# Softplus as one activation in a selective-scan block, its projections one pair earlier

## The chip, the cores and the metric

One Trainium2 chip, one of its cores. The time is the device time of one execution in microseconds (us), the median of several.

## The reference

Input x is (8, 512, 128). The block is x + 0.5 ffn(norm(x)), then x + mamba(norm(x)), then again x + 0.5 ffn(norm(x)). The ffn is a mixture of 16 experts (4 taken per token) and 2 shared ones. The part that the change touches is the mamba block:

```python
x = gelu(_dwconv_same(x, K_x, b_x))
z = gelu(_dwconv_same(z, K_z, b_z))
dt, Bm, Cm = split(einsum('bdl,de->ble', x, W_xproj), ...)
delta = softplus(dt @ W_dt + b_dt)
dA = exp(delta * A)                 # A = -exp(A_log), 16 states
h = dA * h + delta * Bm * u         # a scan along the 512 steps
y = sum_n h * Cm + u * D
out = concat(y, z) @ W_out
```

## The kernel before

The three phases follow each other. Channels lie on the 128 partitions, the 512 steps of one of the 8 rows of the batch along the free dimension.

**Expert phases** (`Ffn`): 8 rows x 18 blocks. PE multiplies in split precision (high and low parts, L1031 to L1035 and L1013 to L1015), ACT applies Silu and splits, DVE multiplies, POOL makes the low part. Into the last blocks of the first expert phase the head of the state-space phase is woven by tables of block numbers (`HEAD_PE`, `HEAD_ACT`, `HEAD_DVE`, `HEAD_POOL`): it prepares row 0 and part of row 1.

**State-space phase** (`Mamba`): for each row (called a batch of pairs here, number i) 8 pairs of states, so 64 pairs, numbered g = 8 i + n. For a pair

- PE spreads two rows of B over the partitions (`pe_spread`, L1516, for pair g + 1), into one of two PSUM banks;
- ACT makes the two decays exp(A delta) (`act_decays`, L1321, for pair g + 2);
- DVE multiplies delta u into the spread B (the input product, `dve_input`, L1435) and scans both states (L1465);
- POOL multiplies the states by C (L1236);
- PE sums them with an identity (the state sum, `pe_add_states`, L1528, for pair g - 3).

Between the pairs PE computes what the row after next needs: the convolutions of x and z as four tap matmuls each (L1493, n = 1 to 6), the transposes of the row three on (L518, at n = 6), the output projection of the row before (n = 4), and, at n = 0, the projections of B and C (`pe_bc`, L1501) and of delta (`pe_delta`, L1506) for row i + 1, into the two halves of the PSUM tile `front`. ACT at n = 7 copies the transposed row to x_pad (L1245) and applies both gelus for row i + 2 (`act_gelus`, L1262 to L1269) out of `front`, with a load of the gelu table before and of the exp table after. B, C and delta are projected from the gelu of x (u), and delta's projection overwrites the convolution of z, so it waits for the gelu of z too (`z_gated`). For row 2 the gelus of the two raw z of rows 0 and 1 are made along with it (L1267).

Softplus has no single step: ACT (`act_soft`, n = 0, 1 and 2) makes |v|, relu(v), e = exp(-|v|), four squares and four affine factors of a polynomial for log(1 + e); POOL (`pool_soft`, n = 3, 4 and 5) multiplies e by the four, adds relu, and multiplies by u for du. For row 0 this is done in the head, by ACT and DVE, and there ACT also makes the decay rates -exp(A_log).

Each engine works off its instructions strictly in order; the order is what the loops in `pe_pairs`, `act_pairs`, `dve_pairs` and `pool_pairs` write down. The lines that decide the order at n = 0 are

```python
if n == 0 and i + 1 < BATCH:
    ...
    self.pe_bc(pe, i + 1, front[:, 0, :])
    need(pe, self.z_gated, i + 2 if i else 0)
    self.pe_delta(pe, i + 1, front[:, 1, :])
```

Of the kernel before, what the change touches and what calls it, by code (L numbers as in the profile page):

```python
# [12 lines left out]
P = 128  # L13
# [18 lines left out]
RING = 4  # L32
# [7 lines left out]


LOG1P = ((1.009357526868805, 1.1060679102671753), (-0.08225465651132796, 3.2574848537500833),
         (-1.4247416849819245, 2.7021171047885773), (-2.3216944609803276, 0.4324090385033215))
LOG1P_SCALE = 0.00523258431847857
# [22 lines left out]
def program(nc, x_in, w_in, w_xproj, w_dt, b_dt, a_log, d_skip, w_out, k_x, b_x, k_z, b_z,  # L67
            router_w, route_bias, gate_w, up_w, down_w, sh_gate_w, sh_up_w, sh_down_w, out):
    ctx = ExitStack()
    with ctx:  # L70
# [75 lines left out]
        log_consts = sb("log_consts", [P, 2 * len(LOG1P)])  # L146
# [116 lines left out]
HEAD_DVE = (101, 102, 104, 106, 107, 109, 110, 116, 118, 134, 135, 136, 137)  # L263
HEAD_POOL = (102, 107, 117, 129)
HEAD_ACT = (105, 106, 109, 113, 117, 120, 124, 125, 128, 131, 132, 133, 135, 137)
# [7 lines left out]
class Setup:  # L273
# [4 lines left out]
    SMALL = 13  # L278

    def __init__(self, nc, ctx, m):  # L280
# [14 lines left out]
        self.a_step = sem("a_step")  # L295
# [25 lines left out]
    def load_rest(self, sp):  # L321
# [9 lines left out]
                 (m["d_sb"][:, :], m["d_skip"]), (m["a_log_sb"][:, :], m["a_log"])]  # L331
# [77 lines left out]
    def dve_consts(self, dve):  # L409
        nc, m = self.nc, self.m  # L410
        zero = Steps(dve, self.consts, 0)
        zero.do(nc.vector.memset(m["same_tile"][:], 1.0))
        zero.do(nc.vector.memset(m["comb"][:], 0.0))
        for n, (a, b) in enumerate(LOG1P):
            if n == len(LOG1P) - 1:
                b *= LOG1P_SCALE
            zero.do(nc.vector.memset(m["log_consts"][:, 2 * n:2 * n + 1], a))
            zero.do(nc.vector.memset(m["log_consts"][:, 2 * n + 1:2 * n + 2], b))
        zero.settle()
        zero.do(nc.vector.memset(m["same_tile"][:, :, 0:1], 0.0))  # L420
        zero.settle()
# [19 lines left out]
    def act_decay_rates(self, ae):  # L441

        nc, m = self.nc, self.m
        self.wait_small(ae)
# [87 lines left out]
class Ffn:  # L532
# [161 lines left out]
    def act_front(self, ae):  # L694
        norm, setup = self.norm, self.setup
        self.nc.scalar.preload_act_table_set("silu_and_others")
# [371 lines left out]
    def pe_front_pieces(self, pe):  # L1068
        mamba = self.mamba
        pe.wait_ge(mamba.soft_act, mamba.SQUARES + (BATCH - 2) * mamba.ACT_SOFT + 2)  # L1070
# [51 lines left out]
class Mamba:  # L1122


    ACT_SOFT, POOL_SOFT = 11, 5
    SQUARES = 7
    SOFT_PIECES = (0, 0, 0, 2, 2, 2, 0, 0)

    def __init__(self, nc, ctx, m, setup, norm, c_dram, f1):
# [9 lines left out]
        assert (RING + 2) * size + SEQ <= NE * 3 * P  # L1139
        sg, act = m["sg"], m["act"]  # L1140
        last = room[:, (RING + 2) * size:(RING + 2) * size + SEQ]
        self.soft_bufs = sg[:, 0], sg[:, 1], act[:, 0], (sg[:, 0], act[:, 1], m["out_t"][:, :], last)
        s, d = self.staged, self.decay
        self.first_bufs = s[:, 0, 0], s[:, 0, 1], s[:, 1, 0], (s[:, 0, 0], s[:, 1, 1], d[:, 3, 0], d[:, 3, 1])
# [11 lines left out]
        self.soft_act, self.soft_mul, self.du_ready = sem("soft_act"), sem("soft_mul"), sem("du_ready")  # L1156
# [37 lines left out]
    def pool_soft(self, pool, r):  # L1194
        nc, m, q = self.nc, self.m, r % 2
        _, relu, e, factors = self.soft_bufs
        count = Steps(pool, self.soft_mul, r * self.POOL_SOFT)
        for n, factor in enumerate(factors):
            pool.wait_ge(self.soft_act, self.SQUARES + r * self.ACT_SOFT - len(factors) + n + 1)
            count.settle()  # L1200
            count.do(nc.gpsimd.tensor_tensor(e, e, factor, ALU.mult))
            yield
        count.settle()
        count.do(nc.gpsimd.tensor_tensor(m["delta"][:, q], e, relu, ALU.add))  # L1204
        assert count.n == self.POOL_SOFT
        yield
        count.settle()
        nc.gpsimd.tensor_tensor(m["du"][:, q], m["delta"][:, q], m["u"][:, r % 3], ALU.mult).then_inc(self.du_ready, 1)
        yield
# [11 lines left out]
    def pool_pairs(self, pool):  # L1221
        nc, m = self.nc, self.m
        for i in range(BATCH):
            softening = self.pool_soft(pool, i + 1)
            for n in range(PAIRS):
                g = i * PAIRS + n
                if i + 1 < BATCH:
                    if n == 1:
                        self.pool_low_rows(pool, i + 1)
                    for _ in range(self.SOFT_PIECES[n]):  # L1230
                        next(softening)
# [27 lines left out]
    def act_gelus(self, ae, r):  # L1259
# [11 lines left out]
        nc.scalar.preload_act_table_set("exp_and_others")  # L1271
# [10 lines left out]
    def act_soft(self, ae, r, src, then=None):  # L1282
        nc, m = self.nc, self.m
        absolute, relu, e, factors = self.soft_bufs if r else self.first_bufs
        s = Steps(ae, self.soft_act, self.SQUARES + (r - 1) * self.ACT_SOFT if r else 0)
        ae.wait_ge(self.dt_ready, r + 1)
        need(ae, self.du_ready, r)
        s.do(nc.scalar.activation(absolute, src, ACT.Abs, bias=m["b_dt_sb"][:, 0:1]))
        s.do(nc.scalar.activation(relu, src, ACT.Relu, bias=m["b_dt_sb"][:, 0:1]))
        s.settle()  # L1290
        if then:
            yield
        s.do(nc.scalar.activation(e, absolute, ACT.Exp, scale=-1.0))
        if then:
            self.setup.act_decay_rates(ae)
            nc.scalar.preload_act_table_set(then)
        yield
        s.settle()
        for n, factor in enumerate(factors):
            s.do(nc.scalar.activation(factor, e, ACT.Square, bias=m["log_consts"][:, 2 * n:2 * n + 1]))  # L1300
        s.settle()
        yield
        if r == 0:
            return
# [7 lines left out]
    def act_decays(self, ae, g):  # L1312
# [3 lines left out]
        if n == 0:  # L1316
            ae.wait_ge(self.soft_mul, (i + 1) * self.POOL_SOFT)
# [343 lines left out]
```

## Time and profile before

| | us |
|---|---|
| median of 3 runs | 932.56 (931.9 to 933.38) |
| the profiled execution | 931.41 |
| its span | 929.3 |
| busy: PE, DVE, POOL, ACT | 887.6, 733.9, 646.3, 576.0 |
| share of the span: PE, DVE, POOL, ACT | 96%, 79%, 70%, 62% |

The first expert phase lasts to about 358 us, the state-space phase to about 604, the second expert phase to the end. PE's granted clock is at or near full speed over most of the span.

How to read the rows below. A timeline row is: start, length (of all its instructions together, where it ends in x2 or more), engine, line, operation, what is written and read, shapes, count; in brackets how long the engine had been idle before, and who released it. A row of stretches is: from and to, length, then the busy time (and count) of PE, of PE's weight loads, of DVE, ACT and POOL, then PE's granted clock as a share of full speed, the DMA engines' share and GB/s. A row of the waits is: who waited for whom, us in total, times, the longest. One fp32 matmul is two records of PE. The ends of matmuls are modelled.

### The profile page before, as it was taken

The page shows a single profiled execution, that of the slowest core. Times are in us where ns is not written, and L with a number is a line of the kernel's source. Part 1 is how long each engine was busy: PE and PEld are TensorE (multiplying, and loading weights), DVE is VectorE, ACT ScalarE, POOL GpSimd, SP SyncE. Part 2 cuts the span into 40 slices and gives each one's busy share as a digit, 9 for nine tenths or more (in the row PEclk, how much of TensorE's full clock was granted, in tenths as well). Part 3 has the DMA queues.
Part 4 walks back from the last instruction along what each step waited for, and adds up shares of the span by engine and source line. Part 5 has one row for each costly group of instructions (what it writes and reads, how often), then busy time and mean ns, then how long its engine had stood idle before and what let it go on. Part 6 is the DMA issues. An engine that isn't in the chain of part 4 may idle for free. (4 is left out here: it accounts for less than half of the span.)

```text
span 929.3 us, 12347 instructions
## 1 busy us (share of the span) xinstructions
PE 887.6 (96%) x3655; PEld 632.7 (68%) x3655; DVE 733.9 (79%) x1248; ACT 576.0 (62%) x1022; POOL 646.3 (70%) x471
## 2 busy tenths in 40 slices
PE   8899999999998999999999887789999999999997
PEld 7678778787766665355455433367878878788885
DVE  5969768777975468999999999956877787796664
ACT  6475565565553778888977594136557557555554
POOL 7658666675655456999999887546666667566665
PEclk9999999999999999999999998999999999999999
DMA  7632443333323223334444344243334343334430
GB/s 201 200 123 78 143 121 95 112 118 100 110 84 90 71 81 112 137 118 160 157 154 141 117 136 137 70 141 122 108 111 133 95 134 114 98 102 138 136 112 13
DMA packets 65587, 109.80 MB, mean 118 GB/s; under 512 B 8168, under 2 KB 24688, under 8 KB 65520
## 3 DMA queue, kind: packets, MB, share of 16 engines
q1 hardware_dynamic: 65520, 109.02, 37.5%
q8 instruction: 29, 0.48, 0.2%
q14 instruction: 38, 0.31, 0.1%
HBM read 106.10 MB, written 2.88 MB: 117 GB/s over the span
## 5 line engine op out<-in xcount | busy, mean ns | idle before, releaser
L654 POOL TENSOR_TENSOR act_lo<-act,act_hi 128x512 fp32r<-128x512 f32 x288 | 374.8, 1303 | 237.9 <-ACT act_hi L745 237.4
L738 ACT ACTIVATE bank<-bank 128x512 f32<-128x512 f32 x252 | 146.6, 582 | 234.5 <-PE bank L1035 226.1
L943 DVE TENSOR_TENSOR sg<-bank,c_ring 128x512 f32<-128x512 f32 x252 | 172.6, 685 | 105.0 <-ACT bank L738 103.8
L1031 PE MATMUL bank<-x_parts,w_hi 128*128 128x512 f32 x572 | 235.8, 412 | 9.7 <-DVE act L923 7.1
L923 DVE TENSOR_TENSOR act<-sg,bank 128x512 f32<-128x512 f32 x288 | 197.8, 687 | 48.7 <-PE bank L1035 33.6
L1035 PE MATMUL bank<-x_parts,w_hi 128*128 128x512 f32 x572 | 225.8, 395 | 0.0
L1032 PE MATMUL bank<-x_parts,w_lo 128*128 128x512 f32 x572 | 225.7, 395 | 0.0
L745 ACT ACTIVATE act_hi<-act 128x512 fp32r<-128x512 f32 x288 | 179.4, 624 | 1.2 <-DVE act L923 0.4
L1031 PEld LDWEIGHTS bank<-x_parts,w_hi 128*128 128x128 f32 x572 | 107.8, 188 | 44.7 <-DVE act L923 14.7
L1035 PEld LDWEIGHTS bank<-x_parts,w_hi 128*128 128x128 f32 x572 | 107.7, 188 | 25.4
L1032 PEld LDWEIGHTS bank<-x_parts,w_lo 128*128 128x128 f32 x572 | 108.0, 189 | 24.5 <-issue 2.6
L1321 ACT ACTIVATE stage<-delta,a_neg 128x511 f32<-128x511 f32 x128 | 83.5, 711 | 53.4 <-POOL delta L1204 38.2
L1013 PE MATMUL bank<-act_hi,w_hi 128*128 128x512 f32 x288 | 114.5, 398 | 2.1 <-POOL act_lo L654 2.1
L1015 PE MATMUL bank<-act_lo,w_hi 128*128 128x512 f32 x288 | 113.7, 395 | 0.0
L1014 PE MATMUL bank<-act_hi,w_lo 128*128 128x512 f32 x288 | 113.5, 394 | 0.0
L1236 POOL TENSOR_TENSOR stage<-stage,c_ring 128x1024 f32<-128x1024 f32 x32 | 75.4, 2366 | 13.7 <-DVE stage L1465 13.6
L1236 POOL TENSOR_TENSOR states<-states,c_ring 128x1024 f32<-128x1024 f32 x32 | 75.7, 2365 | 11.0 <-DVE states L1465 11.0
L1435 DVE TENSOR_TENSOR bank<-du,bank 128x1024 f32<-128x1024 f32 x64 | 77.2, 1207 | 2.8 <-PE bank L1516 2.7
L1465 DVE TENSOR_TENSOR_SCAN states<-stage,bank 128x1024 f32<-128x1024 f32 x32 | 73.1, 2283 | 2.2
L1465 DVE TENSOR_TENSOR_SCAN stage<-stage,bank 128x1024 f32<-128x1024 f32 x32 | 72.9, 2278 | 1.1
L1516 PE MATMUL bank<-bc_parts,sel_n 128*128 128x512 f32 x128 | 55.6, 516 | 15.1 <-DVE stage L1465 12.0
L1528 PE MATMUL bank<-states,ident 128*128 128x512 f32 x128 | 64.5, 630 | 3.6 <-DVE y_sb L1443 3.6
(182 smaller groups left out, 1049.9 us busy)
## 6 DMA issues: line engine op xcount, KB each, us to landing
c_ring<-c_dram SPq DMA_DIRECT2D x252, 256.0 KB, 3.3
c_ring<-c_dram SPq DMA_DIRECT2D x64, 512.0 KB, 3.7
out<-x_sb SPq DMA_DIRECT2D x8, 256.0 KB, 2.7
x_sb<-in_L_attn_hidden_states SPq DMA_DIRECT2D x3, 512.0 KB, 6.0
stage<-in_L_ffn_gate_w SPq DMA_DIRECT2D x4, 256.0 KB, 4.7
stage<-in_L_ffn_up_w SPq DMA_DIRECT2D x4, 256.0 KB, 4.9
stage<-in_L_ffn_down_w SPq DMA_DIRECT2D x4, 256.0 KB, 5.4
c_dram<-c_rows SPq DMA_DIRECT2D x64, 8.0 KB, 1.9
```

The costliest lines, as they stand in the source:

```text
L654: self.nc.gpsimd.tensor_tensor(m["act_lo"][:, g % LAG], m["act"][:, g % ACTS], m["act_hi"][:, g % LAG].bitcast(FP32), ALU.subtract).then_i ...
L738: nc.scalar.activation(self.s_bank[:, g % 2], self.h_bank[:, g % 2], ACT.Silu).then_inc(self.sg_ready, 1)
L745: nc.scalar.activation(m["act_hi"][:, j % LAG], m["act"][:, j % ACTS], ACT.Copy).then_inc(self.hi_ready, 1)
L923: self.nc.vector.tensor_tensor(m["act"][:, g % ACTS], m["sg"][:, g % 2], self.u_bank[:, g % 2], ALU.mult).then_inc(self.act_ready, 1)
L943: nc.vector.tensor_tensor(m["sg"][:, g % 2], silu, weight, ALU.mult).then_inc(self.w_done, 1)
L1013: nc.tensor.matmul(self.acc, hi, m["act_hi"][:, j % LAG], start=first, stop=False, skip_group_check=True)
L1015: nc.tensor.matmul(self.acc, hi, m["act_lo"][:, j % LAG], start=False, stop=last, skip_group_check=True).then_inc(self.down_done, 1)
L1031: nc.tensor.matmul(dst, m["w_hi"][:, k, n, :], x_hi, start=True, stop=False)
L1032: nc.tensor.matmul(dst, m["w_lo"][:, k, n, :], x_hi, start=False, stop=False)
L1035: return nc.tensor.matmul(dst, m["w_hi"][:, k, n, :], x_lo, start=False, stop=True)
L1236: nc.gpsimd.tensor_tensor(self.state(g), self.state(g), m["c_ring"][:, 2 * (n % RING):2 * (n % RING) + 2], ALU.mult).then_inc(self.mul_don ...
L1465: nc.vector.tensor_tensor_scan(flat(self.state(g)), flat(self.decay[:, g % RING]), flat(self.b_bank[g % 2][:]), 0.0, ALU.mult, ALU.add).th ...
```

## The change

1. Softplus is one ACT activation `Softplus` with a table set of its own, out of PSUM into `delta`. ACT's other ten operations and POOL's (in the head DVE's) five are gone; POOL keeps the product du, at n = 2. The constants are gone.
2. The projections of row i + 2 move from n = 0 of the next batch to n = 7 of batch i, behind the spread of that pair and ahead of its state sum. ACT reads them there too (`act_delta`): copies of B and C, softplus. For row 1 they stay at the first pair.
3. The decay rates are made at the very start by ACT, from a DMA that ACT issues itself.

```diff
     def act_decay_rates(self, ae):
-
-        nc, m = self.nc, self.m
-        self.wait_small(ae)
+        nc, m = self.nc, self.m
+        ae.dma_start(m["a_log_sb"][:, :], m["a_log"]).then_inc(self.a_loaded, 16)
+        nc.scalar.preload_act_table_set("exp_and_others")
+        ae.wait_ge(self.a_loaded, 16)
...
-    def act_soft(self, ae, r, src, then=None):
...
+    def act_soft(self, ae, r, src):
+        m = self.m
         ae.wait_ge(self.dt_ready, r + 1)
+        need(ae, self.du_ready, r - 1)
+        self.nc.scalar.activation(m["delta"][:, r % 2], src, ACT.Softplus, bias=m["b_dt_sb"][:, 0:1]
+                                  ).then_inc(self.delta_ready, 1)
+
+    def act_delta(self, ae, r):
+        nc = self.nc
+        nc.scalar.preload_act_table_set("softplus")
+        self.act_parts(ae, r, self.front[:, 0, :])
+        self.act_soft(ae, r, self.front[:, 1, :])
+        nc.scalar.preload_act_table_set("exp_and_others")
...
     def act_pairs(self, ae):
...
-                if n == 0 and i + 1 < BATCH:
-                    self.act_parts(ae, i + 1, self.front[:, 0, :])
-                    next(softening)
-                if n in (1, 2) and i + 1 < BATCH:
-                    next(softening)
+                if g == 0:
+                    self.act_delta(ae, 1)
...
                 if n == 7 and i + 2 < BATCH:
                     self.act_gelus(ae, i + 2)
+                    self.act_delta(ae, i + 2)
...
     def pe_pairs(self, pe):
...
                 if g + 1 < ALL_PAIRS:
                     self.pe_spread(pe, g + 1)
+                if n == 7 and i + 2 < BATCH:
+                    self.pe_bc(pe, i + 2, front[:, 0, :])
+                    pe.wait_ge(self.z_gated, i + 3)
+                    self.pe_delta(pe, i + 2, front[:, 1, :])
                 if g >= SUM_LAG:
                     self.pe_add_states(pe, g - SUM_LAG)
```

PE at the end of batch 1, before: transposes, spread (L1516), state sum (L1528), spread, state sum, then the two projections (L1501, L1506).

```order
L518 MATMUL bank<-ident,xn 128x128 [waits norm_xn_ready,mb_x_added]
L518 MATMUL bank<-ident,xn 128x128 x3
L1516 MATMUL bank<-bc_parts,sel_n 128x512 [waits mb_parts_ready,mb_scan_done]
L1516 MATMUL bank<-bc_parts,sel_n 128x512
L1528 MATMUL bank<-states,ident 128x512 [waits mb_mul_done]
L1528 MATMUL bank<-states,ident 128x512
L1516 MATMUL bank<-bc_parts,sel_n 128x512 [waits mb_scan_done]
L1516 MATMUL bank<-bc_parts,sel_n 128x512
L1528 MATMUL bank<-states,ident 128x512 [waits mb_mul_done]
L1528 MATMUL bank<-states,ident 128x512
L1501 MATMUL bank<-u,w_bc 64x512 [waits mb_u_gated]
L1506 MATMUL bank<-u,w_delta 128x512 [waits mb_z_gated]
L1516 MATMUL bank<-bc_parts,sel_n 128x512 [waits mb_scan_done]
```

With the change (the lines are the changed kernel's: L508 transposes, L1450 spread, L1462 state sum, L1435 and L1440 projections):

```order
L508 MATMUL bank<-ident,xn 128x128 [waits norm_xn_ready,mb_x_added]
L508 MATMUL bank<-ident,xn 128x128 x3
L1450 MATMUL bank<-bc_parts,sel_n 128x512 [waits mb_parts_ready,mb_scan_done]
L1450 MATMUL bank<-bc_parts,sel_n 128x512
L1435 MATMUL bank<-u,w_bc 64x512 [waits mb_u_gated]
L1440 MATMUL bank<-u,w_delta 128x512 [waits mb_z_gated]
L1462 MATMUL bank<-states,ident 128x512 [waits mb_mul_done]
L1462 MATMUL bank<-states,ident 128x512
L1450 MATMUL bank<-bc_parts,sel_n 128x512 [waits mb_scan_done]
L1450 MATMUL bank<-bc_parts,sel_n 128x512
L1462 MATMUL bank<-states,ident 128x512 [waits mb_mul_done]
```

Both projections, with their waits for the gelus, now stand ahead of a state sum and of the next spread.

ACT at the same place, before: copy to x_pad, gelu table, gelu of u and of z, exp table, the decays of the pair after next, then the first steps of softplus.

```order
L1245 ACTIVATE x_pad<-bank 128x512 [waits mb_conv_z,norm_xt_ready]
L1262 ACT_TABLE_LOAD
L1262 ACTIVATE u<-bank,b_x_sb 128x512 [waits mb_conv_x]
L1269 ACTIVATE z<-bank,b_z_sb 128x512 [waits mb_conv_z]
L1271 ACT_TABLE_LOAD
L1321 ACTIVATE stage<-delta,a_neg 128x511 [waits mb_scan_done]
L1321 ACTIVATE stage<-delta,a_neg 128x511
L1278 ACTIVATE bc_parts<-bank 64x512 [waits mb_c_stored,mb_parts_ready,mb_bc_ready]
L1280 ACTIVATE bc_rows<-bank 64x512
L1288 ACTIVATE sg<-bank,b_dt_sb 128x512 [waits mb_du_ready,mb_dt_ready]
L1289 ACTIVATE sg<-bank,b_dt_sb 128x512
L1293 ACTIVATE act<-sg 128x512 [waits mb_soft_act]
```

With the change (L1215 copy, L1232 and L1239 gelus, L1260 and L1263 table loads, L1255 softplus, L1274 decays):

```order
L1215 ACTIVATE x_pad<-bank 128x512 [waits mb_conv_z,norm_xt_ready]
L1232 ACT_TABLE_LOAD
L1232 ACTIVATE u<-bank,b_x_sb 128x512 [waits mb_conv_x]
L1239 ACTIVATE z<-bank,b_z_sb 128x512 [waits mb_conv_z]
L1260 ACT_TABLE_LOAD
L1247 ACTIVATE bc_parts<-bank 64x512 [waits mb_c_stored,mb_parts_ready,mb_bc_ready]
L1249 ACTIVATE bc_rows<-bank 64x512
L1255 ACTIVATE delta<-bank,b_dt_sb 128x512 [waits mb_du_ready,mb_dt_ready]
L1263 ACT_TABLE_LOAD
L1274 ACTIVATE stage<-delta,a_neg 128x511 [waits mb_scan_done]
L1274 ACTIVATE stage<-delta,a_neg 128x511
```

The decays of that pair now follow the copies of B and C, softplus and one more table load.

ACT in the head, before:

```order
L1288 ACTIVATE stage<-bank,b_dt_sb 128x512 [waits mb_dt_ready]
L1289 ACTIVATE stage<-bank,b_dt_sb 128x512
L738 ACTIVATE bank<-bank 128x512 [waits f1_w_done,f1_h_ready,mb_soft_act]
L745 ACTIVATE act_hi<-act 128x512 [waits f1_down_done,f1_act_ready]
L1293 ACT_TABLE_LOAD
L1293 ACTIVATE stage<-stage 128x512
L445 ACTIVATE a_neg<-a_log_sb 128x16 [waits small_loaded]
L447 ACTIVATE a_neg<-a_neg 128x16 [waits a_step]
L1296 ACT_TABLE_LOAD
L738 ACTIVATE bank<-bank 128x512 [waits f1_w_done,f1_h_ready]
```

With the change:

```order
L1297 ACT_TABLE_LOAD
L1255 ACTIVATE delta<-bank,b_dt_sb 128x512 [waits mb_dt_ready]
L1299 ACT_TABLE_LOAD
L729 ACTIVATE bank<-bank 128x512 [waits f1_w_done,f1_h_ready]
L736 ACTIVATE act_hi<-act 128x512 [waits f1_down_done,f1_act_ready]
```

The bank that PE's next transposes need is free after a table load and softplus, where it was free after two activations.

## Rows read from the trace of the kernel before

**Rows 1.** Stretches by busy time of each engine: 400 to 430, 550 to 555 us.

```profile
400.00:430.00 30.00, 30.00 (x94) 15.58 (x93) 29.46 (x19) 25.49 (x42) 28.03 (x16) 1.00 0.42 148
550.00:555.00 5.00, 4.19 (x10) 1.82 (x11) 4.91 (x4) 5.00 (x9) 4.09 (x4) 0.66 0.37 124
```

**Rows 2.** The longest entry of the waits, 345 to 616 us.

```profile
ACT stage L1321 <- POOL delta L1204: 38.2, 7, 9.6
```

**Rows 3.** Timeline of DVE: input products (L1435), scans (L1465), a shift (L494).

```profile
391.02 1.21 DVE L1435 TENSOR_TENSOR bank<-du,bank 128x1024 f32<-128x1024 f32 x1
...
417.68 2.29 DVE L1465 TENSOR_TENSOR_SCAN states<-stage,bank 128x1024 f32<-128x1024 f32 x1
419.89 1.21 DVE L1435 TENSOR_TENSOR bank<-du,bank 128x1024 f32<-128x1024 f32 x1
...
446.55 2.29 DVE L1465 TENSOR_TENSOR_SCAN states<-stage,bank 128x1024 f32<-128x1024 f32 x1
...
462.80 0.19 DVE L494 SCALAR_TENSOR_TENSOR shift<-mean_var,rstd 128x8 f32<-128x8 f32 x1
...
477.38 2.29 DVE L1465 TENSOR_TENSOR_SCAN states<-stage,bank 128x1024 f32<-128x1024 f32 x1
...
560.03 1.23 DVE L1435 TENSOR_TENSOR bank<-du,bank 128x1024 f32<-128x1024 f32 x1 [0.63 <-PE bank L1516]
```

**Rows 4.** Timeline of PE around two ends of a batch, and one batch later.

```profile
384.20 0.60 PE L518 MATMUL bank<-ident,xn 128*128 128x128 f32 x4
...
411.67 1.88 PE L1528 MATMUL bank<-stage,ident 128*128 128x512 f32 x4
413.39 1.02 PE L1493 MATMUL bank<-x_pad,w_tap 128*128 128x512 f32 x2
414.25 0.60 PE L518 MATMUL bank<-ident,xn 128*128 128x128 f32 x4
414.60 0.70 PE L1516 MATMUL bank<-bc_parts,sel_n 128*128 128x512 f32 x2
415.15 1.88 PE L1528 MATMUL bank<-states,ident 128*128 128x512 f32 x4
...
417.33 1.88 PE L1528 MATMUL bank<-states,ident 128*128 128x512 f32 x4
...
445.97 1.88 PE L1528 MATMUL bank<-states,ident 128*128 128x512 f32 x4
```

**Rows 5.** Timeline of ACT at the first and the second end of a batch.

```profile
388.44 0.69 ACT L1262 ACTIVATE u<-bank,b_x_sb 128x512 f32<-128x512 f32 x1
...
390.25 0.67 ACT L1269 ACTIVATE z_third<-bank,b_z_sb 128x512 f32<-128x512 f32 x1
...
415.88 0.58 ACT L1245 ACTIVATE x_pad<-bank 128x512 f32<-128x512 f32 x1
416.47 1.28 ACT L1262 ACT_TABLE_LOAD   x1
417.76 0.69 ACT L1262 ACTIVATE u<-bank,b_x_sb 128x512 f32<-128x512 f32 x1
```

**Rows 6.** Timeline of DVE: the shift of the last norms.

```profile
531.10 1.14 DVE L494 SCALAR_TENSOR_TENSOR shift<-mean_var,rstd 128x8 f32<-128x8 f32 x1 [0.93 <-POOL rstd L487]
```

**Rows 7.** Timeline of PE in the head, end of the first expert phase.

```profile
325.44 0.66 PE L1022 MATMUL bank<-ident,out_t 128*128 128x128 f32 x4 [0.96 <-ACT stage L1289]
...
341.31 0.50 PE L1031 MATMUL bank<-x_parts,w_hi 128*128 128x512 f32 x1 [0.63 <-DVE act L923]
```

**Rows 8.** Timeline of DVE and ACT at the start.

```profile
3.59 0.87 DVE L470 BATCH_NORM_STATS2 stats<-x_sb 128x6 f32<-128x128 f32 x4 [1.94 <-DMA x_sb<-in_L_attn_hidden_states]
...
6.56 1.65 ACT L503 ACTIVATE xn<-x_sb,shift,rstd 128x128 f32<-128x128 f32 x4 [4.50 <-DVE shift L494]
```

**Rows 9.** Timeline of PE after pauses.

```profile
534.50 0.72 PE L1516 MATMUL bank<-bc_parts,sel_n 128*128 128x512 f32 x2 [2.27 <-DVE stage L1465]
...
550.26 3.22 PE L1528 MATMUL bank<-states,ident 128*128 128x512 f32 x4 [1.04 <-DVE y_sb L1443]
```

More of the change, by code:

```diff
@@ L1138, in __init__ @@
         self.staged = room[:, RING * size:(RING + 2) * size].rearrange("p (a s l) -> p a s l", a=2, s=2)
[L1139 to L1144, printed above, removed]
+        assert (RING + 2) * size <= NE * 3 * P
         self.bc_rows = m["bc_rows"]
@@ L1192, in pool_low_rows, with pool_du @@
                                      ALU.subtract).then_inc(self.parts_ready, 1)
[L1194 to L1209, printed above, removed]
+    def pool_du(self, pool, r):
+        m = self.m
+        pool.wait_ge(self.delta_ready, r + 1)
+        self.nc.gpsimd.tensor_tensor(m["du"][:, r % 2], m["delta"][:, r % 2], m["u"][:, r % 3], ALU.mult
+                                     ).then_inc(self.du_ready, 1)
     def pool_head(self, pool):
@@ L1229, in pool_pairs @@
                         self.pool_low_rows(pool, i + 1)
-                    for _ in range(self.SOFT_PIECES[n]):
-                        next(softening)
+                    if n == 2:
+                        self.pool_du(pool, i + 1)
                 if n == 2 and i == 3:
@@ L1280, in act_parts @@
         nc.scalar.activation(self.bc_rows[0:4 * NS, :], src[0:4 * NS, :], ACT.Copy).then_inc(self.rows_copied, 1)
[L1282 to L1285 removed]
+    def act_soft(self, ae, r, src):
+        m = self.m
         ae.wait_ge(self.dt_ready, r + 1)
[L1287 to L1304, printed above, removed]
[L1305 to L1310 removed]
+        need(ae, self.du_ready, r - 1)
[7 more added lines that the diff above has]
+        nc.scalar.preload_act_table_set("exp_and_others")
     def act_decays(self, ae, g):
@@ L1343, in act_head @@
         yield
-        softening = self.act_soft(ae, 0, misc, "silu_and_others")
-        next(softening)
-        yield
-        next(softening)
-        yield
-        next(softening)
+        self.nc.scalar.preload_act_table_set("softplus")
+        self.act_soft(ae, 0, misc)
+        self.nc.scalar.preload_act_table_set("silu_and_others")
         yield
@@ L1363, in act_pairs @@
         for i in range(BATCH):
-            softening = self.act_soft(ae, i + 1, self.front[:, 1, :])
             for n in range(PAIRS):
@@ L1387, in dve_head @@
         norm.dve_aggregate(dve, BATCH)
-        nc.vector.memset(self.decay[:, 0:RING - 1, :, 0:1], 0.0).then_inc(self.zeroed, 1)
+        nc.vector.memset(self.decay[:, :, :, 0:1], 0.0).then_inc(self.zeroed, 1)
         yield
```

74 lines of the change are left out of this document (19 added, 55 removed).

## The prediction

> **What bounds the kernel now.** I read the page first, then the stretches, then one batch of the state-space phase engine by engine. The profiled execution took 931.41 us by the clock outside and 929.3 us by its span; the median of the three runs is 932.56, so the sum is made against 931.41 and 1.15 is added at the end.
>
> The page's first part shows PE at 96% over the whole span, so the two expert phases are PE's. The stretch from 400 to 430 us lies in the state-space phase, and there two engines are full [rows 1]: PE 30.00 of 30 us and DVE 29.46 of 30; POOL has 28.03, ACT 25.49. The waits list then tempts: its longest entry is ACT waiting 38.2 us for POOL's delta [rows 2]. But who waits for ACT there? DVE's timeline answers [rows 3]. A pair is one scan of 2.29 and one input product of 1.21, a step of 3.50, and no row of the stretch names a wait: scan 16 at 417.68, product 17 at 419.89. Scan 16 at 417.68 to scan 24 at 446.55 is a batch of eight pairs in **28.87 us**, all of it DVE work; batch 3, which also holds norm statistics, takes 477.38 - 446.55 = 30.83. So ACT's 38.2 us are slack that DVE never sees.
>
> How much slack has PE? In [rows 4] the same place of two successive batches, the state sum after spread 17 and the one after spread 25, stands at 417.33 and 445.97: **28.64 us**, and in the stretch between them I find PE without a gap. So a batch is 28.9 us on DVE and 28.6 on PE. PE can lose 0.2 us a batch, and beyond that only what it can be late within a batch; what it idles beyond that, DVE will wait for.
>
> **The change part by part.**
>
> *Softplus in the pairs.* For each of seven batches 11 ACT operations, some 0.7 us each, become one, and POOL loses five products of the half size. All of that lies beside DVE's chain [rows 2, 3], so it is worth nothing. What it costs is one more table load per batch: gelu, softplus, exp in place of gelu, exp.
>
> *B, C and delta a pair sooner.* This is the term that decides. Before, PE at the last pair of a batch (n = 7) issues spread 16 and sum 12, then at the next pair spread 17, sum 13 and only then the projections. Now the projections stand right behind spread 16, ahead of sum 12 and spread 17, and they wait for the gelus. The gelus are behind something that PE has only just done: the transposes of x, the last thing of n = 6, which go from 414.25 to 414.85 [rows 4]. From there the chain is ACT's [rows 5]: the copy to x_pad, the gelu table and the gelu of u go from 415.88 to 418.45, which is 2.57 us. Before, that chain started late, at 415.88, because ACT had waited for delta; now it can start at once, at 414.9. With 0.05 for each of two handovers B and C's projection starts at 414.85 + 2.67 = 417.52. Without a wait it would start where sum 12 stands now, at 415.15. **PE's gap: 2.4 us.** The gelu of z ends at most its own 0.7 us later, while the first projection (half of 1.72) runs, so delta adds nothing.
>
> Then delta's projection, sum 12 and spread 17 must pass before DVE gets product 17. The projections are two fp32 products like a sum, and a sum takes 1.72 us (411.67 to 413.39). So: 417.52 + 1.72 + 1.72 = 420.96 for spread 17, 0.55 until it is read = 421.5, where DVE wants it at 419.89 [rows 3]: PE's backlog of before plus the gap breaks through at once. From the second boundary on PE is the bound: a batch takes it 28.64 + 2.40 = 31.04 us.
>
> Boundary by boundary. First (batch 0 to 1): transposes end at 384.80 [rows 4]; here two more gelus of z precede the third, which ends 2.48 us after u's starts [rows 5], so delta's projection starts at 384.80 + 1.93 + 2.48 + 0.05 = 389.26. It takes 0.86, sum 4 takes 1.72, spread 9 0.55: 392.4 against 391.02, **+1.4**. Second: PE's next spread at that place is 31.04 after 391.84, so its product can start at 423.4 against 419.89 + 1.4: **+2.1**. Third: 31.04 - 28.87 = **+2.2**. Fourth, behind the long batch 3: 31.04 - 30.83 = **+0.2**. Fifth: **+2.2**. The sixth has no transposes ahead, u's gelu isn't held, and I take 0; it may cost 1.5. Sum **+8.1**.
>
> *ACT behind the gap.* The trace has no softplus; the nearest row is the gelu, from the same bank with the same kind of bias, 0.69 [rows 5]. From the first projection's start at 417.52: gelu z 0.7, softplus table 1.28, two copies at most 0.7 each, softplus 0.7, exp table 1.28, the two decays of pair 18 at 0.7 each: 424.2. Scan 18 stood at 417.68 + 2 x 3.50 = 424.68 and is now later by the stall of 2. Hidden, even at twice the price.
>
> *The late shift.* At 531.10 DVE waited 0.93 us for POOL's root and the shift took 1.14 [rows 6], with a POOL product beside it; the one at 462.80 took 0.19 [rows 3]. POOL has four products less ahead of its root now, so the root comes first. Between 0.9 and 1.9 goes; I take **-1.2**, since a POOL product will probably still stand beside the shift.
>
> *The head, in the first expert phase.* PE's transposes of the output waited for ACT to free the bank, until 325.44 [rows 7]: two operations of the gelu's kind, 1.3 us. Now a table load and softplus, 1.28 + 0.69: +0.7. Later DVE loses five operations; PE had waited 0.63 for DVE there [rows 7]: -0.6. Together **+0.1**.
>
> *The start.* The decay rates move to ACT's front with a DMA of their own. ACT has nothing to do before 6.56 [rows 8]. The DMA is issued at about 0.8; if it lands like x, at 3.6, and the two small operations take no more than an apply each (1.65 / 4 = 0.4), and the second table 1.28, ACT is ready at 5.7. 0.9 us spare: **0**; if the DMA delays x or itself, up to +1. SP issues one small load less, among weight loads that nobody waits for yet.
>
> Sum: 8.1 - 1.2 + 0.1 = **+7.0**. 931.41 + 7.0 = 938.4 for an execution like the profiled one, and **939.6 us** against the median.
>
> **A rule against it.** ACT goes from copy to table load to gelu at 416.46, 416.47 and 417.76 [rows 5]: 1.28 us and no pause around it, and I take 1.28. The Trainium skill (ScalarE: Activation LUTs, What ACT_TABLE_LOAD costs) puts a switch at 1283 ns of load plus some 1380 ns of drain, 2.66 us. The trace has the load and not the drain. By this figure of the Trainium skill each gap would be 1.4 us longer.
>
> **The rivals.** *A, faster:* PE's gap doesn't reach DVE, since PE has more room than its record shows (ends of matmuls are modelled, and it may regain time where I see it full). Then DVE stays the bound, and the shift (-1.9), PE's 0.63 us hold-up of DVE at 560 [rows 3] and the head (+0.1) are what is left: -2.4, **930.2 us**. It decides from a real PE batch below 28.87 - 2.40 = 26.5 us; against it stand the two sums 28.64 apart. Chance 0.09. *B, half of it:* the gap comes partly out of PE's room; a gain and a loss of about 2 us meet: 931 to 934.4, chance 0.06. *C, the clock:* PE's granted clock fell to 0.66 in the stretch 550 to 555, after two pauses with one spread between them, and the sum at 550.26 took 3.22 us in place of 1.88 [rows 1, 9]; after 2.27 us of pause behind full work, at 534.50, it did not fall. The new gap of 2.4 us stands between full stretches like the latter. If it fell at each of five gaps, PE being the bound, that is 1.3 to 1.8 each, 7 to 9 us: **947 us**. Chance 0.12. *D, a slow switch:* the load makes the engine pause once PE waits right behind it, by at most its own length again. Four gaps times 1.28 on top: **944.7 us**. The row of the old load shows no such pause, so chance 0.03. It is what the Trainium skill's section named above speaks for.
> The forecast itself has 0.70.
>
> **How the numbers follow.** The forecast's own range is 936 to 942.5 (sixth boundary 0 to 1.5, shift 0.9 to 1.9, start 0 to 1, the gap 2.2 to 2.6 at four places). Rival A and half of C lie outside a range from 933.5 to 945; that leaves out some 0.2. A measurement of this kernel tells 0.2%, 1.9 us, from no change. Faster by more: A, **0.09**. Slower by more: the forecast, C, D and a little of B, **0.86**. Within: **0.05**.
>
> **What would show it.** Right: PE idle of about 2.4 us ahead of the w_bc product at five places, released by ACT's u; DVE's input product waiting for PE's spread of bc_parts at five places, by 1.4, 2.1, 2.2, 0.2 and 2.2 us; ACT's waits for delta gone; POOL's busy time down by 35 products of 1.27, 44 us, for nothing; PE batches of 31 us. The head's wait at the transposes 0.7 longer. Wrong: DVE batches still 28.9 us (A), or PE's clock under 1 behind the gaps (C), or a pause of more than 0.1 between a table load and the operation behind it (D).

## The result, and the profile after

The changed kernel takes **958.07 us** (median of 4 runs, 955.57 to 958.9) against 932.23 us before (4 runs, 931.6 to 933.38): ratio **1.0271, 95% interval 1.0248 to 1.0294**, 2.7% slower. The prediction had the sign and not the size: 939.6, with a range of 933.5 to 945.

The profiled execution took 958.9 us, its span is 956.8. From the first part of the page:

```profile
span 956.8 us, 12195 instructions
PE 897.0 (94%) x3655; PEld 636.8 (67%) x3655; DVE 732.1 (77%) x1234; ACT 545.2 (57%) x955; POOL 602.9 (63%) x436
```

POOL has 43.4 us less to do than before (646.3) and ACT 30.8 less (576.0). Where is the time? Scan 0 to scan 63, the state-space phase, takes 241.43 us before (360.15 to 601.58) and 267.19 now (363.04 to 630.23): **+25.8**. The first expert phase adds 2.9, the rest of the span takes 1.2 off. So the loss lies between the scans. DVE's timeline at the second end of a batch, columns as in [rows 3]: start, length, what it is, and in brackets the idle time before it with its releaser:

```profile
421.23 2.29 DVE L1399 TENSOR_TENSOR_SCAN stage<-stage,bank 128x1024 f32<-128x1024 f32 x1
423.43 1.21 DVE L1369 TENSOR_TENSOR bank<-du,bank 128x1024 f32<-128x1024 f32 x1
429.46 2.29 DVE L1399 TENSOR_TENSOR_SCAN states<-stage,bank 128x1024 f32<-128x1024 f32 x1 [4.82 <-PE bank L1462]
431.66 1.21 DVE L1369 TENSOR_TENSOR bank<-du,bank 128x1024 f32<-128x1024 f32 x1
```

The product that I expected to be late (431.66, product 17) is on time behind its scan. What stalls is **scan 16, one step earlier**, and its releaser is not the spread but L1462, PE's state sum. There are six such stalls, 4.25, 4.82, 4.84, 2.34, 4.87 and 4.92 us: 26.0 together, the whole loss. In the waits list of 357 to 635 us (line waited for, total, times, longest) they stand in two entries:

```profile
DVE states L1399 <- PE bank L1462: 16.2, 4, 4.8
DVE states L1399 <- ACT stage L1274: 9.8, 2, 4.9
```

The second entry is a releaser put down wrongly. One of its two is the stall at 568.64 (scan 48): the sum ahead of it is on PE from 565.63 for 2.88 us, which is 568.51, and the scan starts right behind it. The other is the stall at 531.03 (scan 40), behind a sum from 527.97 to 530.90.

PE at the same place, to hold against [rows 4]:

```profile
420.55 0.60 PE L508 MATMUL bank<-ident,xn 128*128 128x128 f32 x4
420.90 0.70 PE L1450 MATMUL bank<-bc_parts,sel_n 128*128 128x512 f32 x2
423.83 1.58 PE L1435 MATMUL bank<-u,w_bc 128*64 128x512 f32 x2 [2.23 <-ACT u L1232]
425.34 2.08 PE L1440 MATMUL bank<-u,w_delta 128*128 128x512 f32 x2
427.21 2.12 PE L1462 MATMUL bank<-states,ident 128*128 128x512 f32 x4
428.76 1.03 PE L1450 MATMUL bank<-bc_parts,sel_n 128*128 128x512 f32 x2
429.63 1.88 PE L1462 MATMUL bank<-states,ident 128*128 128x512 f32 x4
431.80 0.74 PE L1450 MATMUL bank<-bc_parts,sel_n 128*128 128x512 f32 x2 [0.30 <-DVE states L1399]
```

Three things are to be seen. The gap ahead of the projection is there, 2.23 us, released by u. Sum 12 at 427.21 comes behind both projections; before it stood at 415.15, right behind spread 16. And the rows behind the gap are long: 1.58 and 2.08 for projections that elsewhere take 1.07 and 1.12. The granted clock says why (columns as in [rows 1]):

```profile
400.00:430.00 30.00, 27.52 (x81) 13.69 (x80) 24.82 (x17) 16.39 (x25) 19.57 (x10) 0.94 0.42 141
424.00:426.00 2.00, 2.00 (x3) 0.52 (x3) 0.64 (x1) 1.97 (x3) 2.00 (x1) 0.57 0.60 217
```

The clock falls so behind five of the six gaps. Behind the fourth it doesn't, though the gap is as long, and the stall there (497.38, scan 32) is 2.34 us, the shortest of the six. It stands behind the long batch 3, which leaves more slack (experiment 4 has no stall there):

```profile
493.40 1.07 PE L1435 MATMUL bank<-u,w_bc 128*64 128x512 f32 x2 [2.20 <-ACT u L1232]
494.40 1.12 PE L1440 MATMUL bank<-u,w_delta 128*128 128x512 f32 x2
```

ACT's side of the gap, against [rows 5]:

```profile
421.18 0.60 ACT L1215 ACTIVATE x_pad<-bank 128x512 f32<-128x512 f32 x1 [3.70 <-PE bank L508]
421.80 1.28 ACT L1232 ACT_TABLE_LOAD   x1
423.09 0.69 ACT L1232 ACTIVATE u<-bank,b_x_sb 128x512 f32<-128x512 f32 x1
423.68 0.68 ACT L1239 ACTIVATE z<-bank,b_z_sb 128x512 f32<-128x512 f32 x1
424.38 1.28 ACT L1260 ACT_TABLE_LOAD   x1
425.67 0.59 ACT L1247 ACTIVATE bc_parts<-bank 64x512 fp32r<-64x512 f32 x1
...
427.45 0.69 ACT L1255 ACTIVATE delta<-bank,b_dt_sb 128x512 f32<-128x512 f32 x1 [0.71 <-PE bank L1440]
```

Copy, table and gelu of u take 2.6 us behind the transposes, softplus (L1255) costs 0.69 like a gelu, and each table load is 1.28 with 0.01 us around it.

The start and the head, against [rows 8] and [rows 7]:

```profile
3.98 0.87 DVE L460 BATCH_NORM_STATS2 stats<-x_sb 128x6 f32<-128x128 f32 x4 [2.52 <-DMA x_sb<-in_L_attn_hidden_states]
```

```profile
6.95 1.65 ACT L493 ACTIVATE xn<-x_sb,shift,rstd 128x128 f32<-128x128 f32 x4 [2.00 <-DVE shift L484]
```

```profile
329.81 0.66 PE L1013 MATMUL bank<-ident,out_t 128*128 128x128 f32 x4 [1.81 <-ACT delta L1255]
```

x lands 0.39 us later, with the first apply (6.95 for 6.56), and the head's wait is 0.85 longer.

**The theory after the result.** A state has one of four buffers. Scan g writes the one of pair g-4, so it waits until PE has summed that state: `need(dve, self.sum_done, g - RING + 1)` in `dve_pairs`. Scan 16 needs sum 12, and sum 12 is what the change put behind the projections. Before, it ended at 415.15 + 1.88 = 417.03 and scan 16 came at 417.68 [rows 4, 3]: 0.65 to spare. Now ahead of it stand the gap, 2.23, and two projections, 1.72 (2.23 + 1.72 - 0.65 = 3.3), and the rest of the 4.82, some 1.5, would be the clock. Rivals: the spread behind the projections, as predicted (rival 2 below); the clock alone (3); softplus and its tables (4).

### The profile page after: what moved, and what is told of

The parts are those of the page before. It is cut to its first block and busy times, and to the rows that moved or that the text cites. A ratio compares the mean times of both kernels' runs of the same rounds, so it can differ in the third digit from the quotient of the medians.

```text
span 956.8 us, 12195 instructions
## 1 busy us (share of the span) xinstructions
PE 897.0 (94%) x3655; PEld 636.8 (67%) x3655; DVE 732.1 (77%) x1234; ACT 545.2 (57%) x955; POOL 602.9 (63%) x436
## 3 DMA queue, kind: packets, MB, share of 16 engines
HBM read 106.10 MB, written 2.88 MB: 114 GB/s over the span
## 5 line engine op out<-in xcount | busy, mean ns | idle before, releaser
L1274 ACT ACTIVATE stage<-delta,a_neg 128x511 f32<-128x511 f32 x128 | 83.8, 712 | 74.8 <-DVE states L1399 40.4
L1450 PE MATMUL bank<-bc_parts,sel_n 128*128 128x512 f32 x128 | 55.0, 511 | 17.9 <-DVE stage L1399 10.3
L1462 PE MATMUL bank<-states,ident 128*128 128x512 f32 x128 | 64.6, 631 | 4.8 <-DVE y_sb L1377 4.8
```

## The experiments

Times are medians, ratios are against the kernel before on the same chip, which took 933.3 to 933.43 us in all these runs.

**1. The sum ahead of the projections.** In `pe_pairs`, against the changed kernel:

```diff
                 if g + 1 < ALL_PAIRS:
                     self.pe_spread(pe, g + 1)
+                if g >= SUM_LAG:
+                    self.pe_add_states(pe, g - SUM_LAG)
                 if n == 7 and i + 2 < BATCH:
                     self.pe_bc(pe, i + 2, front[:, 0, :])
                     pe.wait_ge(self.z_gated, i + 3)
                     self.pe_delta(pe, i + 2, front[:, 1, :])
-                if g >= SUM_LAG:
-                    self.pe_add_states(pe, g - SUM_LAG)
```

> The changed kernel, but at the last pair of a batch the state sum (sum 12) goes ahead of the two projections, not behind them. Theory 1 (DVE's scan 16 stalls for sum 12, which frees its state buffer): sum 12 is done before ACT has u ready, the stall of 4.8 us at six scans goes, PE's gap falls from 2.2 to 0.5 us, PE's clock stays near 1 there; 932 to 937 us. Rival 2 (the recorded prediction: what DVE waits for is spread 17 behind the projections, wherever the sum stands): only the 1.7 us go by which the gap is filled, six times: about 948 us. Rival 3 (the fallen clock is what costs): about 2 us at six places, 946 us. Rival 4 (the softplus, its tables or late decays on ACT): no change, 958 us.

Measured: 933.84 us, ratio 1.0008 (0.9997 to 1.0019). Two calls swapped give back 24 us. PE's timeline at the second end of a batch:

```profile
414.85 0.71 PE L1450 MATMUL bank<-bc_parts,sel_n 128*128 128x512 f32 x2
415.40 1.88 PE L1462 MATMUL bank<-states,ident 128*128 128x512 f32 x4
417.79 1.07 PE L1435 MATMUL bank<-u,w_bc 128*64 128x512 f32 x2 [0.51 <-ACT u L1232]
418.79 1.13 PE L1440 MATMUL bank<-u,w_delta 128*128 128x512 f32 x2
419.35 1.03 PE L1450 MATMUL bank<-bc_parts,sel_n 128*128 128x512 f32 x2
```

The gap is 0.51, as the sum fills 1.7 of it, and the projections run at full clock. DVE has three stalls left in the phase, 0.50, 0.38 and 0.40. Rival 2 (948) and rival 4 (958) fall. Rival 3 can't be judged here, since the gap is gone too.

**2. Softplus without the earlier projections.** The projections go back to n = 0 of the next batch, on PE and ACT alike:

```diff
-                if n == 7 and i + 2 < BATCH:
-                    self.pe_bc(pe, i + 2, front[:, 0, :])
...
-                if g == 0:
+                if n == 0 and i + 1 < BATCH:
...
-                    self.pe_bc(pe, 1, front[:, 0, :])
-                    self.pe_delta(pe, 1, front[:, 1, :])
+                    self.pe_bc(pe, i + 1, front[:, 0, :])
+                    need(pe, self.z_gated, i + 2 if i else 0)
+                    self.pe_delta(pe, i + 1, front[:, 1, :])
```

> The changed kernel with its single softplus, head and start, but the projections where they stood before the change (first pair of the next batch, behind the state sum), with four table loads a batch on ACT. Theory 1: no stall at scans 16 and so on, 931 to 935 us; POOL some 40 us less busy, for nothing. If softplus or its tables cost DVE anything: more than 940 us. If the start and the head cost what the first expert phase shows (up to 2.9 us): 934 to 935.

Measured: 934.18 us, ratio 1.0009 (0.9999 to 1.0018). From scan 0 to scan 63 it takes 241.72 us, as the kernel before (241.43), and no scan waits for a sum. Softplus, four table loads a batch, and 43 us less on POOL are worth nothing, either way.

**3. The earlier projections without softplus.** The kernel before with the block of PE moved as in the change:

```diff
+                if n == 7 and i + 2 < BATCH:
+                    self.pe_bc(pe, i + 2, front[:, 0, :])
+                    pe.wait_ge(self.z_gated, i + 3)
+                    self.pe_delta(pe, i + 2, front[:, 1, :])
                 if g >= SUM_LAG:
                     self.pe_add_states(pe, g - SUM_LAG)
-                if n == 0 and i + 1 < BATCH:
-                    if i == 0:
...
+                if g == 0:
```

> The kernel before with one part of the change: the projections of B, C and delta issued at the last pair of a batch, ahead of the state sum; the polynomial softplus shared with GpSimd stays. Theory 1: the whole loss comes with this part, and a little more, since ACT starts its copy, table and gelu 1 us later behind its wait for delta: 958 to 966 us. If the loss were softplus's own: 932 us. By the recorded prediction's own sizes (+8.1): 941 us.

Measured: 962.61 us, ratio 1.0314 (1.0297 to 1.0331). The stalls are at the same places, 7.91, 3.34, 5.05, 4.83, 5.00 and 4.98 us ahead of scans 8 to 48, and one of 0.38 later. From its waits:

```profile
DVE states L1465 <- PE bank L1528: 31.5, 7, 7.9
```

So the moved projections carry the loss, with softplus or without it. The first stall is the longest because PE's gap there is 3.95 us. At scan 16, with 3.34, the clock stayed up behind a gap of 2.38 us: the projections took 1.07 and 1.13.

**4. The gelus ahead of the copy of x.** The order on PE stays as in the change; on ACT, u's gelu no longer waits behind a copy that waits for PE's transposes:

```diff
+                if n == 7 and i + 2 < BATCH:
+                    self.act_gelus(ae, i + 2)
                 if n == 7 and i + 3 < BATCH:
                     self.act_copy_xt(ae, i + 3, self.misc)
                 if n == 7 and i + 2 < BATCH:
-                    self.act_gelus(ae, i + 2)
                     self.act_delta(ae, i + 2)
```

> The changed kernel, but ACT does the gelus of u and z ahead of its copy of the next x, so that they no longer wait for PE's transposes. PE's gap of 2.2 us goes and its clock stays at 1; the state sum is still behind the projections. Theory 1: sum 12 then ends some 0.5 us after scan 16 is due, six stalls of about 0.5 us, none of 4.8: 933 to 938 us. If the order on PE (two projections more ahead of the sum) cost it by itself, without the gap: 1.7 us six times stays, about 943 us. If the tables or softplus on ACT do: 958 us.

Measured: 940.48 us, ratio 1.0077 (1.0059 to 1.0096), above what I expected by 2.5. The stalls are 0.45, 0.88, 0.87, none, 0.89, where about 0.5 was told, and then 3.69. DVE's timeline at scans 16 and 48:

```profile
421.37 2.29 DVE L1400 TENSOR_TENSOR_SCAN states<-stage,bank 128x1024 f32<-128x1024 f32 x1 [0.88 <-PE bank L1463]
...
549.12 2.29 DVE L1400 TENSOR_TENSOR_SCAN states<-stage,bank 128x1024 f32<-128x1024 f32 x1 [3.69 <-PE bank L1463]
```

0.88 us is the price of the order alone: two projections, 1.72, less some 0.8 of slack (0.65 by [rows 4, 3]). The sixth boundary is another matter, and PE's timeline shows it:

```profile
540.87 0.73 PE L1451 MATMUL bank<-bc_parts,sel_n 128*128 128x512 f32 x2 [2.15 <-DVE stage L1400]
543.58 1.97 PE L1436 MATMUL bank<-u,w_bc 128*64 128x512 f32 x2 [1.98 <-ACT u L1232]
```

There u is late for another reason. ACT's table and gelus stand behind an apply that had waited 5.82 us for DVE's shift, and PE, with two pauses in a row, is at half its clock: 1.97 us for a product of 1.07.

**5. The gap filled with work.** Against the changed kernel, whose order and late gelu stay:

```diff
                 if n == 7 and i + 2 < BATCH:
+                    for _ in range(2):
+                        self.nc.tensor.matmul(self.y_acc, self.m["zeros"][:, :], self.m["u"][:, i % 3],
+                                              start=False, stop=False, skip_group_check=True)
                     self.pe_bc(pe, i + 2, front[:, 0, :])
```

> The changed kernel with PE's gap filled: two fp32 products with a zero tile, 1.7 us, added to the open sum of y (they add nothing) between spread 16 and the projection of B and C; the order, and u's late gelu, stay. It separates the clock from the gap. Theory 1 with rival 3 as its second part (of the 4.8 us of a stall, 2.8 is the order and the gap, 2.0 the clock that falls behind 2.2 us of idle PE): the projections run at 1.07 and 1.12 us, six stalls of about 2.8 to 3.2, in all 946 to 949 us. If idling has nothing to do with the clock: stalls of 4.8 and 958 us. If the stall were all clock: 935 us.

Measured: 949.61 us, ratio 1.0174 (1.016 to 1.0187). That is 0.6 above the range expected. Useless work, put where PE idled, makes the kernel 8.5 us faster. PE and DVE at the second end of a batch:

```profile
419.10 1.88 PE L1531 MATMUL bank<-u,zeros 128*128 128x512 f32 x4
421.48 1.07 PE L1437 MATMUL bank<-u,w_bc 128*64 128x512 f32 x2 [0.51 <-ACT u L1234]
422.48 1.12 PE L1442 MATMUL bank<-u,w_delta 128*128 128x512 f32 x2
423.45 1.88 PE L1464 MATMUL bank<-states,ident 128*128 128x512 f32 x4
```

```profile
425.46 2.29 DVE L1401 TENSOR_TENSOR_SCAN states<-stage,bank 128x1024 f32<-128x1024 f32 x1 [3.17 <-PE bank L1464]
```

The stall is 3.17 in place of 4.82. So the 4.82 come apart: order 0.88 (experiment 4), gap 2.29 (3.17 - 0.88; it measures 2.23), clock 1.65. By the medians of the whole kernels: order and the sixth boundary 7.2 us (940.48 against 933.32 of the next kernel), gaps 9.1 (949.61 - 940.48), clock 8.5 (958.07 - 949.61). By the profiles, from scan 0 to scan 63 alone (242.38, 248.81, 259.99 and 267.19 us), it is 6.4, 11.2 and 7.2. The clock's price between the scans is thus 7.2 us. In the profiles another 1.6 us of the difference lies ahead of scan 0 (361.42 against 363.04), where the filler changes nothing.

The fourth boundary is the control: there the clock had not fallen, and the filler leaves the stall as it was, 2.33 us for 2.34. At the sixth the filler came too late, since it ran at half the clock itself (3.23 us in place of 1.88), and the stall is 3.44.

**6. Both orders mended** (1 and 4 together).

> The changed kernel with the state sum ahead of the projections and the gelus ahead of the copy of x. Theory 1: no gap on PE, no stall of DVE at scan 16 or product 17; 1.3 us less than the kernel with the sum ahead alone (its three stalls of 0.4 to 0.5): 932 to 933 us, against 933.4 of the kernel before. If two projections together ahead of spread 17 cost DVE by themselves, 1 us a boundary: 939 us.

Measured: 933.32 us, ratio 1.0003 (0.9994 to 1.0012). In the profile one stall for a sum is left, 0.42 us. It confirms the cause and wins nothing: with the projections harmless, DVE's batch is what it was.

**7. The start undone as well.** `a_log` among SyncE's loads, the decay rates behind softplus in the head:

```diff
-        ae.dma_start(m["a_log_sb"][:, :], m["a_log"]).then_inc(self.a_loaded, 16)
-        nc.scalar.preload_act_table_set("exp_and_others")
-        ae.wait_ge(self.a_loaded, 16)
+        self.wait_small(ae)
...
         self.act_soft(ae, 0, misc)
+        self.nc.scalar.preload_act_table_set("exp_and_others")
+        self.setup.act_decay_rates(ae)
```

> The kernel with both orders mended, with one more part of the change undone: a_log among SyncE's small loads and the decay rates in the head, behind softplus, as before. If the DMA and the table load at ACT's front cost what the first norm's apply shows, 0.4 us: 0.4 less than the kernel with both orders mended. If they are what lets PE's clock fall in the stretch 30 to 60 us (0.94 in three profiles with this start, 1.00 in a fourth): 1 to 2 us less. If the start costs nothing: the same, or 1.3 more for a third table load in the head.

Measured: 931.82 us, ratio 0.9993 (0.9983 to 1.0002). Its interval overlaps that of experiment 6, so the start isn't shown to cost anything. Nor is it what drops PE's clock in the stretch from 30 to 60 us: that was 0.94 in the profiles of experiments 2, 4 and 6 and 1.00 in those of 1, 5 and 7, but experiments 9 and 10, with the start of before, have 1.00 and 0.89.

**8. The freed time put to use.** On top of experiment 6, DVE's skip term goes for seven of the eight batches: ACT copies the sum of y, and PE adds D*u in the output projection through a weight scaled by D. To make room on PE, POOL adds up the two states of a pair, for two pairs a batch:

```diff
+                if g in HALVED:
+                    pool.wait_ge(self.mul_done, g + 1)
+                    halves = self.state(g)
+                    nc.gpsimd.tensor_tensor(halves[:, 0], halves[:, 0], halves[:, 1], ALU.add
+                                            ).then_inc(self.halved, 1)
...
+                nc.tensor.matmul(self.misc[:, cols], m["u"][:, i % 3][:, cols], m["w_skip"][:, :], start=False, stop=False)
...
-                if i and n == 2:
-                    self.dve_skip_term(dve, i - 1)
```

> Meant to beat both: both orders mended, and the time that the single softplus frees on ACT and POOL put to use. DVE's skip term (y + D*u, 0.74 us and 0.65 of its chain, seven times) goes: ACT copies the sum of y instead (0.6), and PE takes D*u through a weight scaled by D, four products of 128x128 more in the output projection (0.9 us a batch). POOL adds the two halves of the states of two pairs a batch (1.27 each), so that PE sums one product for them, not two (1.7 us a batch less). If DVE is the bound: 0.65 x 7 = 4.6 us less than the kernel with both orders mended, 927 to 929 us. If PE is, as its 28.64 against 28.87 allows: 28.64 - 0.8 leaves room, so 930 at worst. If POOL, now with two adds more, gets late with the states (its pair has 1.1 us to spare, two adds and du need 3.8 + 0.7 of 9): about the same as before, 932.

Measured: 930.52 us, ratio 0.9967 (0.9955 to 0.9979). It gives 2.8 us against experiment 6, not 4.6: DVE's batch (scan 14 at 412.71, scan 22 at 441.12) is 28.41 us, which is 0.46 less than 28.87, not 0.65. It misses the 927 to 929 of the case that DVE is the bound.

**9. The same, with the start of before, and the two late shifts on POOL.** In `pool_root`, for these two places:

```diff
+            nc.gpsimd.tensor_tensor(m["shift"][:, q, :], m["mean_var"][:, q, :, 0], m["rstd"][:, q, :], ALU.mult
+                                    ).then_inc(self.product_ready, 1)
+            pool.wait_ge(self.product_ready, 1 if r == BATCH + 6 else 2)
+            nc.gpsimd.tensor_scalar(m["shift"][:, q, :], m["shift"][:, q, :], -1.0, None, ALU.mult
+                                    ).then_inc(self.shift_ready, rows)
```

> The kernel that puts the freed time to use, with the start and the decay rates as before the change, and the norm's shift of the two late places made by POOL (two small operations behind its root) in place of DVE. In its profile the shift at 532.33 took 2.23 us behind a wait of 0.77 on DVE, while a large product ran on POOL. If DVE's small operation is held by what POOL runs beside it: 3 us off DVE's chain there, and about 1 at the later place; with 1.5 for the start, 930.5 - 4 to 5.5 = 925 to 926.5 us. If POOL's two small operations come as late and ACT's apply then holds the transposes: 929 us.

Measured: **926.81 us, ratio 0.9930 (0.9915 to 0.9945)**, the fastest kernel of the study, below both the kernel before and the changed one. The phase from scan 0 to scan 63 takes 237.20 us (experiment 8: 239.33; before: 241.43). The time is 0.3 above the range expected.

**10. DVE's second operation of a batch moved too.** PE adds x through the identity, ACT writes it back, and POOL adds up the states of four pairs a batch.

```diff
+                nc.tensor.matmul(self.misc[:, cols], m["ident"][:, :], m["x_sb"][:, i, t, :], start=False, stop=False)
...
-                if i and n == 5:
-                    self.dve_add(dve, i - 1)
+                if i and n == 5:
+                    self.act_x(ae, i - 1)
```

> The same, and DVE's second operation a batch goes too: PE adds x to the output projection through the identity (four products of 128x128 more, 0.9 us a batch), ACT copies the sum to x, and POOL halves the states of four pairs a batch, not two. DVE's batch is 8 x 3.50 = 28.0 us in place of 28.4, seven times: 2.9 less, 922 to 924 us, if DVE stays the bound. PE's batch by sums: 28.64 + 0.9 + 0.9 - 4 x 0.86 = 27.0, below it. POOL's: 8 x 2.37 + 2 x 1.26 + 4 x 1.27 = 26.6 of 28: if POOL gets late with its products instead, DVE stalls for sums and it is slower than the kernel above.

Measured: 930.83 us, ratio 0.9978 (0.9966 to 0.999), 4.0 slower than experiment 9 where I expected 3 to 5 faster. DVE waits 0.27 us for a sum in four of the batches, and the late stretch, where PE idles most, has a clock of 0.82 (experiment 9: 0.86; here the rows of both, 10 first):

```profile
550.00:580.00 30.00, 20.64 (x86) 11.54 (x86) 28.18 (x35) 13.10 (x23) 21.81 (x12) 0.82 0.39 130
```

```profile
550.00:580.00 30.00, 22.01 (x83) 11.94 (x82) 29.35 (x42) 11.62 (x19) 19.95 (x10) 0.86 0.40 133
```

But that isn't where the 4.0 us are. The phase takes 237.10 us in its profile, as in experiment 9 (237.20). The first expert phase ends 2.3 us later, with a clock of 0.89 between 30 and 60 us, and what follows scan 63 takes 1.7 us longer (328.21 against 326.52). Why these two parts are longer stays open.

**11. The late shifts on POOL in the kernel before**, the edit of 9 alone.

> The kernel before with one edit: the two late shifts on POOL in place of DVE. It measures the term 'the late shift' of the prediction, 0.9 for the wait and 1.1 for the operation: if both lay on DVE's chain, 931.4 to 932.5 (1 to 2 us less). If PE's batch of 28.64 or the phase's end takes it back: no change, 933.4.

Measured: 933.63 us, ratio 1.0006 (0.9995 to 1.0018): no gain. In its profile (936.41 us, at the upper end of its runs, 931.69 to 936.62) DVE loses the time again right behind, waiting for PE: batch 5, which holds the shift, is 2.1 us shorter (30.83 against 32.90), batch 6 is 5.5 longer (38.67 against 33.17).

```profile
558.18 1.23 DVE L1444 TENSOR_TENSOR bank<-du,bank 128x1024 f32<-128x1024 f32 x1 [2.67 <-PE bank L1525]
```

So the shift was not on a path that DVE alone sets. Taken off in the kernel before it moves the wait to PE; experiment 9 is 3.7 us faster than experiment 8. By the profiles 2.1 of them lie between scan 0 and scan 63, behind the start and the head, so these go to the shifts. What the rest is isn't settled.

## Why the prediction was wrong in size

**What bounds.** Right: DVE's 28.87 us a batch, PE close behind, ACT's and POOL's time without worth. Experiment 2 shows it.

**The gap.** Right: 2.4 us forecast, 2.20 to 2.23 measured at the five places told and from the cause told; experiment 4 removes the cause, and these five gaps are gone. A sixth of 1.98, at the last boundary, has another cause (see below).

**What waits for it: the step that failed.** "Then delta's projection, sum 12 and spread 17 must pass before DVE gets product 17." I listed sum 12 as mere length on the way to spread 17, and didn't ask who waits for sum 12 itself. Scan 16 does, through the ring of four states, and it comes 2.2 us before product 17. With the term's own numbers, and the 0.65 of slack from [rows 4, 3], it would have been 2.23 + 1.72 - 0.65 = 3.3 us at the second boundary; experiment 5, at full clock, has 3.17. The rows were there: sum 12's end 0.65 us ahead of scan 16 is a wait that shows no idle time because it is met just in time.

**The series over the boundaries.** Wrong for the same reason. I let PE be the bound, so that a stall was only 31.04 - 28.87 and nearly nothing at the long batch 3. But behind each stall PE waits for DVE (0.30 at 431.80), so its lateness isn't carried over, and each boundary pays its own stall: 4.25, 4.82, 4.84, 2.34, 4.87, 4.92 in place of 1.4, 2.1, 2.2, 0.2, 2.2, 0. The sixth, taken as 0, has no transposes ahead, but u's gelu is held by the apply, which waits 5.82 us for the shift:

```profile
556.93 1.65 ACT L493 ACTIVATE xn<-x_sb,shift,rstd 128x128 f32<-128x128 f32 x4 [5.82 <-DVE shift L484]
```

**Rival C, the clock.** Given 0.12 as an alternative; it came on top: 1.65 us at the second boundary, in the 1.3 to 1.8 I had put on it, and 7.2 us between the scans, by the profiles. I had held one pause against it, 2.27 us at 534.50 [rows 9] with no fall behind it. That happens in the changed kernel too, at the fourth boundary, but only at one of six. One such row was too little.

**Rival D, the slow switch.** Refuted: 0.01 us between a table load and the operation behind it, with PE waiting right there. Here the measurement decides against the figure in the Trainium skill (ScalarE: Activation LUTs, What ACT_TABLE_LOAD costs), whose load of 1283 ns the trace has, and whose drain of some 1380 ns it doesn't. **Rivals A and B** fell with the six stalls.

**ACT behind the gap, hidden.** Right; experiment 1 has no stall for decays.

**The late shift, -1.2.** The root came in time, as told, but the shift itself got longer: 0.19 and 1.14 before [rows 3, 6], 1.50 and 2.03 after:

```profile
554.87 2.03 DVE L484 SCALAR_TENSOR_TENSOR shift<-mean_var,rstd 128x8 f32<-128x8 f32 x1
```

```profile
554.53 2.35 POOL L1206 TENSOR_TENSOR states<-states,c_ring 128x1024 f32<-128x1024 f32 x1
```

It ends at 556.90, with POOL's product (556.88). The other shift (479.32, 1.50 us) ends at 480.82, again with a product of POOL (478.43 + 2.36 = 480.79), and for it the prediction had no term: in experiment 2, where no scan waits for a sum, batch 3 takes 32.05 us against 30.83 [rows 3]. Over the whole phase experiment 2 is 0.3 us longer than the kernel before, where 1.2 less was forecast.

**The head and the start.** The head's wait grew by 0.85 (0.7 forecast). The start cost 0.39 in the trace (0, with up to 1); what it is worth in the end is not shown. Scan 0 came 2.9 us later in the profile, but in that of experiment 1, with the same start and head, only 0.36 (360.51). A part of it falls in the stretch from 30 to 60 us, where the clock was 0.94 against 1.00 before, and that comes and goes among kernels that are the same there.

**The range.** The terms named for the forecast's own range, added up, give 938.1 to 943.2, not 936 to 942.5. The result lies far outside both.

## What to carry to other kernels

When work is put ahead of an operation on one engine, list everybody who waits for that operation, ring buffers first: a release that arrives 0.65 us early shows no idle time, and yet it is a deadline that 1.7 us of work put ahead of it breaks. An in-order engine that is made to wait can pay three times: the wait, the work that was moved ahead of the urgent one, and, on PE, the clock behind the pause. Freed time on an engine that nobody waits for is worth nothing until work is moved onto it from the bounding engine. Measure the whole kernel then: experiment 10's batches are 0.2 us shorter than experiment 9's, and its time is 4.0 longer.

## What the runs showed of the hardware

- PE's clock behind a pause of some 2.2 us among full stretches falls to half at five boundaries of six in the changed kernel: the rows go from 1.07 and 1.12 us up to 1.97 and 2.08, with a granted clock of 0.57 from 424 to 426 us. It stays up at the fourth behind 2.20 us, in experiment 3 once behind 2.38, and before behind 2.27 [rows 9]. What makes the difference is not shown. 1.7 us of products with zeros in the pause keep it up at the first five (experiment 5).
- DVE's tiny shift (128x8) doesn't end before the large product that POOL is working on: 554.87 + 2.03 = 556.90 against 554.53 + 2.35 = 556.88, and in experiment 8 532.33 + 2.23 = 534.56 against 532.20 + 2.34 = 534.54. DVE's scans and products beside the same POOL products keep their 2.29 and 1.21.
- ACT's single Softplus from a bank with a bias takes 0.69 us for 128x512, the same as Gelu.
